# An attention and feed-forward kernel: row loads, column centring and one transpose moved to other places and other engines

## The reference

```python
x = x + attention(layernorm(x), Wq, bq, Wk, bk, Wv, bv)      # 16 heads of 64
x = x + layernorm(x) @ (weight * scale[:, None]).T + bias
# attention: each block of 128 queries sees a window of 256 keys around it;
# and for each head the first token, the last one and the 62 tokens with the largest |q|
# attend to all 1024 keys, and overwrite their rows of the result
```

## Time and profile before

| what | value |
|---|---|
| median of three runs | 2242.39 us |
| the profiled execution's own time | 2242.39 us |
| its span, first to last instruction | 2240.8 us |
| PE busy | 2166.2 us (97%), mean granted clock 0.982 |
| DVE busy | 1486.8 us (66%) |
| ACT busy | 827.8 us (37%) |
| POOL busy | 596.1 us (27%) |
| chain that ended last | PE 87%, DVE 6%, DMA 2%, issue 2%, ACT 2% |
| HBM traffic | 78 GB/s over the span |

### The profile page before, as it was taken

One profiled execution on the slowest core, in us unless ns is written; L12 is line 12 of the kernel. 1 busy time (PEld: TensorE's weight loads), 2 busy tenths in 40 slices (PEclk: granted clock), 3 DMA queues, 4 the chain that ended last, 5 costly groups with the idle time before them and its releaser, 6 DMA issues.

```text
span 2240.8 us, 38387 instructions
## 1 busy us (share of the span) xinstructions
PE 2166.2 (97%) x12768; PEld 1849.1 (83%) x12768; DVE 1486.8 (66%) x2989; ACT 827.8 (37%) x2186; POOL 596.1 (27%) x464
## 2 busy tenths in 40 slices
PE   5999999999999989999999999999999978999999
PEld 4888887888888878888888787888888877888887
DVE  6587676664876766748777666396666566666664
ACT  2334444452354444532544455325445450000000
POOL 1332232124322321243213212433132103212221
PEclk9999999999999999999999999999999978999999
DMA  3332112113322121133121211321121113333331
GB/s 141 94 97 70 61 50 78 52 31 122 96 64 67 50 77 52 31 117 99 62 70 50 77 49 34 97 80 44 52 77 43 33 50 126 140 131 125 137 140 66
DMA packets 116723, 175.35 MB, mean 78 GB/s; under 512 B 16208, under 2 KB 81814, under 8 KB 116624
## 3 DMA queue, kind: packets, MB, share of 16 engines
q1 hardware_dynamic: 108688, 155.25, 21.3%
q10 hardware_dynamic: 4608, 16.78, 1.8%
q0 software_dynamic: 3328, 2.17, 0.6%
HBM read 122.73 MB, written 51.44 MB: 78 GB/s over the span
## 4 chain that ended last, share of the span: by engine, by line
PE 87%; DVE 6%; DMA 2%; issue 2%; ACT 2%; POOL 0%; SPq 0%; DVEq 0%; POOLq 0%; ACTq 0%
PE proj L512 42%; PE proj L784 15%; PE pv L635 10%; PE turn L625 5%; PE score L610 4%; PE pv L679 3%; PE score L660 2%; DMA stat_rows<-ln_rstd 1%; PE turn L775 1%; PE misc L647 1%; PE turn L670 1%; PE turn L553 1%; DVE xT_lo L1136 1%; ACT xT_hi L825 1%; DVE top_idx L1177 0%
## 5 line engine op out<-in xcount | busy, mean ns | idle before, releaser
L512 PE MATMUL proj<-xT_hi,w_hi 128*128 128x512 f32 x1536 | 404.2, 405 | 6.5 <-DVE xT_lo L1136 5.4
L512 PE MATMUL proj<-xT_hi,w_lo 128*128 128x512 f32 x1536 | 409.7, 398 | 0.0
L512 PE MATMUL proj<-xT_lo,w_hi 128*128 128x512 f32 x1536 | 381.2, 390 | 0.0
L512 PEld LDWEIGHTS proj<-xT_lo,w_hi 128*128 128x128 f32 x1536 | 288.4, 188 | 62.4
L512 PEld LDWEIGHTS proj<-xT_hi,w_lo 128*128 128x128 f32 x1536 | 283.0, 189 | 63.2 <-issue 0.5
L512 PEld LDWEIGHTS proj<-xT_hi,w_hi 128*128 128x128 f32 x1536 | 277.3, 190 | 62.1 <-issue 6.0
L897 ACT ACTIVATE probs<-score,neg_max 128x256 f32<-128x256 f32 (+1 forms) x512 | 228.7, 459 | 184.4 <-DVE neg_max L1224 120.4
L405 POOL TENSOR_TENSOR ctx_out<-pv_sum,row_inv 128x256 f32<-128x256 f32 x128 | 84.1, 657 | 677.5 <-DVE pv_sum L1261 659.7
L381 POOL CAST w_hi<-w_raw 128x1024 fp32r<-128x1024 f32 x96 | 113.8, 1186 | 524.0 <-PE proj L512 365.3
L383 POOL TENSOR_TENSOR w_lo<-w_raw,w_hi 128x1024 fp32r<-128x1024 f32 x96 | 231.6, 2412 | 7.8
L635 PE MATMUL pv<-v_nat,pT_hi 128*128 128x128 f32 x1024 | 200.2, 278 | 15.3 <-DVE pT_lo L1240 15.3
(11 more groups left out here) (147 smaller groups left out, 3461.1 us busy)
## 6 DMA issues: line engine op xcount, KB each, us to landing
w_raw<-in_wstream SPq DMA_DIRECT2D x96, 512.0 KB, 3.9
x_buf<-in_rows SPq DMA_DIRECT2D x56, 512.0 KB, 3.3
q_rows<-q_nat SPq DMA_DIRECT2D x64, 256.0 KB, 3.0
ctx_rows<-ctx_out SPq DMA_DIRECT2D x128, 128.0 KB, 1.8
q_store<-ctx_rows SPq DMA_DIRECT2D x32, 512.0 KB, 4.2
out<-q_store ACTq DMA_DIRECT2D x32, 512.0 KB, 2.6
q_store<-in_cols SPq DMA_DIRECT2D x28, 512.0 KB, 4.0
q_store<-in_rows SPq DMA_DIRECT2D x8, 512.0 KB, 5.3
```

Source lines behind the costliest of these rows:

```text
L512: mm = pe.matmul(proj[:, bank, :], w[b][:, k * P:k * P + P], x[:, k, half * HALF:half * HALF + HALF], start=(m == 0), stop=(m == 23), skip ...
```

## The change

The change has these parts:

1. **Row loads on SP.** `load_rows(n, 1)` after the Q stores is gone. Units 0 to 2 are now a hardware loop in which the row loads stand *before* `stores`: column load, rows of pair hp + 1, then `stores`. The last column is loaded in unit 4 (it was unit 2), and the statistics are spread at the start of unit 5, before its stores (they were spread after the stores of unit 3).
2. **Row moments on DVE.** `row_moments(n, 0)` moves from the Q phase to the end of unit 0, pairs 1 to 3 to the ends of units 1 to 3, and `row_roots` from the end of unit 3 to that of unit 4.
3. **Column steps.** SCALE_AT moves from units 4 to 6, (4,1) to (6,1), to units 5 and 6, (5,3) to (6,3). The subtraction of the mean moves from DVE to GpSimd (`centre`, in units 5 and 6). LO_AT and HI_AT are spread a little later in unit 7.
4. **GpSimd order in unit 4.** `store_rows`, `load_columns` and `gather` now all stand ahead of unit 4's `split_key`. `split_key` used to stand between the first and the second.
5. **Top rows.** The 24 finds of the second half are spread 3, then 5, 5, 5, 6 over units 0 to 3 (before 3, then 6, 6, 6, 3), so that `top_rows(n, 1)` is at the end of unit 3 (before: in its middle). `split_q` of unit 0 goes ahead of `top_rows(n, 0)`.
6. **PE head.** `turn_early_q(n, 1, 0)` now stands in the middle of `project_half(n, 2, 0)` at the end of `head`. It used to follow it, as the first thing in `rest`.

```diff
+        SCALE_AT = {(5, 3): (0,), (5, 4): (1, 2), (5, 6): (3, 4), (6, 0): (5,), (6, 1): (6,), (6, 3): (7,)}
+        LO_AT = {(6, 5): (0, 1), (6, 6): (2, 3, 4, 5, 6, 7), (7, 1): (0, 1, 2), (7, 2): (3, 4, 5), (7, 3): (6, 7)}
...
-                if following:
-                    load_rows(n, 1)
                 apart(sp)
-                for hp in range(PAIRS):
+                with sp.Fori(0, HALF_PAIRS - 1) as hp:
+                    load_column(n, hp)
+                    if following:
+                        load_rows(n, hp + 1)
+                    stores(n, hp, [wstream[PAIRS + 4 + 2 * hp], wstream[PAIRS + 5 + 2 * hp]])
+                for hp in range(HALF_PAIRS - 1, PAIRS):
                     if hp < KC - 1:
                         load_column(n, hp)
+                    if hp == HALF_PAIRS:
+                        load_last_column(n, following)
+                        if not following:
+                            spread_scale(n)
+                    if hp == HALF_PAIRS + 1 and following:
+                        spread_stats(n)
...
-                    if hp < 2 and following:
-                        load_rows(n, hp + 2)
...
+            def centre(n, ks):
+                for k in ks:
+                    i = COLS.index(k)
+                    if i == 0:
+                        pool.wait_ge(stat_in, n * 32 + 32)
...
+                    pool.tensor_tensor(column(k), column(k), mean_b, ALU.subtract).then_inc(col_centred, 1)
...
                 for s in range(STEPS - 1):
                     normalise(n, hp, s)
+                    centre(n, cols[s])
                 if value:
                     split_value(n, hp)
                 normalise(n, hp, STEPS - 1)
+                centre(n, cols[STEPS - 1])
...
-                unit(n, HALF_PAIRS, second_half=True)
-                unit(n, PAIRS - 3)
-                unit(n, PAIRS - 2, value=following)
+                store_rows(n, 1)
+                load_columns(n, 1)
+                gather(n, 1)
+                apart(pool)
+                unit(n, HALF_PAIRS)
+                unit(n, PAIRS - 3, cols=(COLS[0:1], COLS[1:3], COLS[3:5], COLS[5:7]) if following else ((),) * STEPS)
+                unit(n, PAIRS - 2, value=following, cols=(COLS[7:8], (), (), ()) if following else ((),) * STEPS)
...
-                project_half(n, 2, 0)
+                project_half(n, 2, 0, (0,))
+                turn_early_q(n, 1, 0)
+                project_half(n, 2, 0, (1,))
...
-                if following and hp < HALF_PAIRS - 1:
-                    row_moments(n, hp + 1)
-                if following and hp == HALF_PAIRS - 1:
+                if following and hp < HALF_PAIRS:
+                    row_moments(n, hp)
+                if following and hp == HALF_PAIRS:
                     row_roots(n)
```

More of the change, by code:

```diff
@@ L255, in load_column @@
                 apart(sp)
-                sp.dma_start(q_store[:, k, :],
+                sp.dma_start(q_store[:, bass.ds(k, 1), :].rearrange("p a c -> p (a c)"),
                              cols_in[n * KC + k + KC]).then_inc(col_in, 16)
@@ L437, in gather, with unit @@
                                             ).then_inc(sel_in[half], 16)
-            def unit(n, hp, key=True, value=True, second_half=False):
-                if second_half:
-                    store_rows(n, 1)
+            def centre(n, ks):
[3 more added lines that the diff above has]
+                        pool.wait_ge(stat_in, n * 32 + 32)
+                    if k == KC - 1:
+                        pool.wait_ge(last_col_in, n * 16 + 16)
+                    else:
+                        pool.wait_ge(col_in, n * (16 * (KC - 1)) + 16 * k + 32)
+                    apart(pool)
+                    pool.tensor_tensor(column(k), column(k), mean_b, ALU.subtract).then_inc(col_centred, 1)
+            def unit(n, hp, key=True, value=True, cols=((), (), (), ())):
                 if key:
                     split_key(n, hp)
-                if second_half:
-                    load_columns(n, 1)
-                    gather(n, 1)
                 for s in range(STEPS - 1):
                     normalise(n, hp, s)
+                    centre(n, cols[s])
                 if value:
@@ L1379, in batch @@
                         norm_of(n, 2 * j + b, h)
-                if following:
-                    row_moments(n, 0)
                 for j in range(PAIRS // 4, PAIRS // 2):
@@ L1387, in batch @@
                             top_find(n, 0, step)
+                split_q(n * PAIRS, 0)
                 top_rows(n, 0)
                 k_lo_out(n, 0, 0)
-                split_q(n * PAIRS, 0)
                 top_find(n, 1, 0)
@@ L1395, in batch @@
                 k_lo_out(n, 0, 1)
-                attend(n, 0, 0, range(3, 9), following)
-                attend(n, 1, 0, range(9, 15), following)
-                attend(n, 2, 0, range(15, 21), following)
-                attend(n, 3, 0, range(21, TOP_STEPS), following)
+                attend(n, 0, 0, range(3, 8), following)
+                attend(n, 1, 0, range(8, 13), following)
+                attend(n, 2, 0, range(13, 18), following)
+                attend(n, 3, 0, range(18, TOP_STEPS), following)
                 for hp in range(HALF_PAIRS, PAIRS):
```

29 lines of the change are left out of this document (9 added, 20 removed).

## The result

The changed kernel takes 2360.53 us (median of 4 runs, 2355.22 to 2361.51), the kernel before 2242.18 us (4 runs, 2238.35 to 2242.73). The ratio is 1.0527, with a 95% interval of 1.0508 to 1.0546: slower by 118 us, where 2370 us was predicted. The profiled execution took 2358.95 us.

The account below looks back on a forecast made before the run. TensorE, busy for 97% of the span, was taken as the bound, so only its gaps and added work count. Terms: 2242.4 + 108 (A) + 16 (B) + 10 (C) + 19.5 (E) - 25.4 (D) = 2370 us; range 2300 to 2420.

Parts of the forecast that it names:

- A: SP's queue: value split late for part 0 of units 1 to 3, batches 0 to 2; nine times, 108 us slower.
- the clock's price: Extra TensorE time at the lowered clock behind a gap: 3.7 us for a long gap, 2.1 us for a short one.
- The store behind the slice: Step 0's store on SP lands about 0.5 us behind the raw value slice; upper bound 1.8 us, 15 us more.
- B: Unit 4's key split comes late for TensorE's part 2, in all four batches: 16 us slower.
- the index store lands some 2.3 us later: Unit 4 on GpSimd: the index store lands 2.3 us after the indices are set at 327.0, ahead of the column loads.
- long index wait: Rival, 15%: 8.5 us idle at unit 4's key split, so 49 us instead of 16, and 2403 us.
- C: Heads of the next batch: TensorE waits about 2.8 us for the q_nat copy, 10 us slower for two heads.
- D: Unit 4 of the three looped batches: VectorE's wait for the spread statistics goes, saving 25.4 us.
- E: GpSimd's subtractions hold back VectorE's multiplications at (5,4) and (5,6), two delays a batch: 19.5 us slower.
- the statistics' wait only moves: Rival, 8%: the spread lands too late in unit 5, (5,3) waits as (4,1) did, the saving is lost: 2395 us.
- `split_q` at nothing: Moving split_q costs nothing, covered by VectorE's 12 idle us a unit.
- The queue doesn't hide it: Rival, 5%, that the queue hides: the value split ends before 202.52, only the statistics' saving matters, 2217 us.

Follow-up runs that it names:

- experiment 2: Kernel before, with SP's row loads ahead of the stores in units 0 and 1: 2311.13 us, ratio 1.0311.
- experiment 3: Changed kernel with the raw value slice issued ahead of the row loads in SP's loop, the stores still behind them: 2343.79 us, ratio 1.0465.
- experiment 11: Kernel before with only its table of column steps (SCALE_AT) later, first at (4,3), never two columns at one place: 2213.26 us, ratio 0.9876.
- experiment 12: Kernel before with experiment 11's table, and unit 6's columns in LO_AT and HI_AT up to one place earlier: 2210.81 us, ratio 0.9873.
- experiment 5: Changed kernel with row loads behind the stores, and unit 4's GpSimd order, the early transpose and split_q put back as before: 2243.32 us, ratio 1.0017.
- experiment 9: Experiment 5's kernel with store_rows, load_columns and gather ahead of unit 4's split again, and the last batch's scale writes and loads one place later: 2256.64 us.
- experiment 6: Experiment 5's kernel with the subtraction of the mean back on VectorE, at the same later places: 2241.62 us, ratio 1.0012.
- experiment 10: Experiment 5's kernel with the finds ended in the middle of unit 3 instead of at its end: 2237.01 us, ratio 0.9989.
- experiment 1: Changed kernel with the row loads of SP's loop put back behind the stores, all else as changed: 2272.17 us, ratio 1.0137.

## Why the prediction was right

The wait of each of the five terms is in the trace, and the sum was 9.5 us too high (2370 against 2360.5). It is that near in part by luck: A was 20 us too high, and the three places that had been put at nothing (`kT_lo`, unit 7, `v_nat` in unit 4) took 5.3, 3.7 and 7.2 us.

- **A: right, the size 20 us too high.** The steps stand as predicted. Rows were due at 198.15 and came at 199.09, the slice's landing was put 5.9 us behind its issue and took 6.2, and GpSimd's normalise, cast and subtraction were put at 4.5 us (0.6 and 3.9) and took 4.0. But the time at which TensorE wants the split had moved further than the rows' time. I took 202.52 from the kernel before, and the changed one reached part 0 only at 203.97 (211.64 - 7.67), 1.45 us later, the rows 0.94 us later. So the idle time is 7.7 us here and 7.5 us in the mean of the nine, not 8.3. The larger miss is the clock's price: 2.3 us a gap (87.9 / 9 - 7.5), not 3.7. The term that was mis-sized is this price, and the traces show why. Only the part of the low clock that lies behind a gap costs time. In the kernel before, 6.8 to 8.4 us at 0.50 lay behind the three gaps of unit 4, and they cost 3.3 to 4.1 us, half of it. In the nine gaps of the changed kernel the clock had fallen 2.7 to 5.3 us before the gap's end, 3.3 to 6.2 us at 0.50 lay behind it, and the price was 1.8 to 3.2 us, again half. The gaps of 9.5 us in experiment 2 cost 2.9 and those of 5.65 us in experiment 3 cost 2.3 in the mean.
- **The store behind the slice.** I took 0.5 us behind the slice's landing, and it was 207.57 against 207.15, 0.4 us. By the page "DMA: Bandwidth & Descriptors" of the Trainium skill ("Anatomy of one DMA") most of the fixed cost is the receipt of the last write. That section describes a DMA from GpSimd's queue, and this store stands on SP's. By it I had put the store up to 1.8 us behind the slice; the trace has it 0.4 us behind, so the 1.8 us did not come on top.
- **B: right in kind, batch 3 wrong.** Three batches had 2.5 to 2.8 us of idle (predicted 1.8), and B's own part is 14.5 us of the 21.7 in the table, against 16. The failed step is "the index store lands some 2.3 us later", which batches 0 to 2 keep and batch 3 doesn't: 6.3 us of wait, for 7.55 us of idle. I had put the danger into the column loads (the rival "long index wait", 2403 us). Their wait was 2.5 to 3.8 us in all four batches. I didn't test what made the 9.16 us of the earlier trace rows, but the traces narrow it down. The wait is 8.3 to 10.4 us in the looped batches of experiments 2, 11 and 12, where the statistics are spread ahead of unit 4 as before, and 2.5 us in experiment 5, where they are spread in unit 5 and GpSimd's order in unit 4 is as before. So the order on GpSimd doesn't make it, and the later column steps of experiment 11 don't take it away. What is left is the statistics' way with the moments and the last column's load, which moved along with it. The idle time of batch 3 came near that rival's 8.5 us by another cause, and experiment 9 shows which: the loads ahead of the index store.
- **C: right.** 2.5 and 2.2 us at the transpose, near the predicted 2.8, 1.2 and 1.1 more at the next one, and none at the third head; 7.7 against 10. ScalarE's gap before the copy (5.31 us in the earlier trace rows) is there in the changed kernel as well, with 4.92 us.
- **D: right in unit 4.** VectorE waits nowhere for the statistics, and unit 4's 25.4 us are gone. But experiments 5 and 6 show that the steps moved into units 5 and 6, with `top_rows` at the end of unit 3, take the same again. I had that as E, a cost of its own. It is rather D's second half: what a wait gives back in unit 4 must be free of charge where its work goes. The rival "the statistics' wait only moves" fell. GpSimd does wait for them in unit 5, up to 3.8 us, so that its first subtraction fits with less room than I gave it, but VectorE's first multiplication is not held.
- **E: the size right (20.7 against 19.5) in part by luck, the cause half.** Units 5 and 6, which the term was about, took 17.0 us. The other 3.7 are unit 7, which I had counted as unchanged: TensorE waits 3.0 us for `xT_lo` there, where it waited 1.8. The long multiplications are there, up to 3.42 us, and GpSimd's own subtractions go from 2.4 to 3.4 us beside them. The rule of the Trainium skill cited there (GPSIMD Engine Reference, "Architecture"), that GpSimd's ports are shared with VectorE, agrees with these times. But experiment 6 shows that without GpSimd's part the time is within 2 us of the same. The step that failed is that E is the price of GpSimd's subtraction beside VectorE: with all of VectorE's steps at these places and the subtraction on VectorE, units 5 to 7 cost the same. The two columns at one place are the likely cause, which is argued and not shown; `top_rows` is not, by experiment 10.
- **`split_q` at nothing: wrong.** I named VectorE's idle time in a unit as its cover, but its place is ahead of unit 0, where VectorE is busy with the finds. Ahead of `top_rows` and of `k_lo_out` it delays `kT_lo`, which the last projection ahead of unit 0 waits for: 1.3 to 1.4 us, four times.
- **The queue doesn't hide it** (rival, 5%): the split ended 7.7 us behind the time at which TensorE wanted it. Experiment 1, where the queue is out of the way, takes 2272 us and not 2217, since B, C, E and `kT_lo` are left.

## What to carry to other kernels

In a queue with one order, a wait costs what stands behind it. Before a wait is moved ahead, list the transfers behind it, and ask of each who reads it next and when; here a buffer that VectorE frees at a unit's end came to hold the weights of the next unit's first matmul. Where an engine waits for a result, first try to move the first user later by a few microseconds, one step at a place: that was one line here, and 28 us. And the price of a long gap in clock is half of the time at 0.50 that lies behind the gap, so read both from the trace, the gap's end and the end of the low clock.

## What was not expected of the hardware

- A small store to memory is as slow as the loads around it. The step's store (128 KB) of 1.8 us took 5.9 us from SP's row (201.69) to GpSimd's start behind it (207.57), with three 512 KB loads ahead. The index store (4 KB, on GpSimd's own queue) kept GpSimd waiting for 6.3 us instead of 2.1 when four of them had just been issued on SP's queue, and for 3.85 us with three and more distance.
- Gaps of 5.7 us and of 7.5 us cost the same in clock in the mean, 2.3 us, and less than gaps of 4.2 to 5.7 us in unit 4 of the kernel before (3.3 to 4.1 us). There the granted clock fell nearer to the gap's end (from 2.9 us ahead of it to 0.2 us behind it), so more of the time at 0.50 fell on work.
- Beside GpSimd's work even a small instruction of VectorE takes microseconds: `g_ctx` (128x64) 2.36 us, where the same instruction took 0.26 us in experiment 6.
- ScalarE stands still for 4.92 us at the back edge of the batch loop, with nothing shown as its wait (5.31 us before, and none at batch 3's head). The DMA records have instruction fetches inside these gaps (two of 8 KB at 549.3 in the one of 4.92 us, which ends at 551.37) and none of that kind at batch 3's head. That fits an engine that waits for its code; no run tests it.
